# Two layers in one kernel on one core: first-round decays, one transform and the first trunk norm moved in their queues

## What is computed

```python
x = L0_attn_x                                   # 2 x 1024 tokens, 512 features, fp32
x = _layernorm(x + _L0_attn_ref(...))           # chunked linear attention with per-head decay,
                                                #   group RMS norm, sigmoid gate, Wo
x = _layernorm(x + _L0_ffn_ref(x, W1, W2, W3))  # silu(x W1) * (x W3), Hadamard transform of the
                                                #   2048 hidden features, W2
x = _layernorm(x + _L1_attn_ref(...))           # selective scan, 32 states for each feature
x = _layernorm(x + _L1_ffn_ref(...))            # silu(gate) * up, down
```

## Time and profile before

| | us |
|---|---|
| median of 3 runs | 1839.29 (1838.42 to 1845.17) |
| the profiled execution, its own time | 1843.79 |
| its span, first to last instruction | 1842.0 |
| TensorE busy | 1756.0 (95%) |
| VectorE busy | 1242.6 (67%) |
| ScalarE busy | 1119.2 (61%) |
| GpSimd busy | 1190.7 (65%) |

### The profile page before, as it was taken

How to read it: one execution, slowest core, us unless ns; L and a number is a source line. 1 busy time by engine, 2 the same in 40 slices (tenths; PEclk the granted TensorE clock), 3 DMA queues, 4 the chain that set the end, 5 groups by cost and what they waited for, 6 DMA issues and landing times. The chain is left out here.

```text
span 1842.0 us, 26738 instructions
## 1 busy us (share of the span) xinstructions
PE 1756.0 (95%) x9472; PEld 1132.3 (61%) x9472; DVE 1242.6 (67%) x1336; ACT 1119.2 (61%) x1721; POOL 1190.7 (65%) x932
## 2 busy tenths in 40 slices
PE   7898989889989999999999999998999999999998
PEld 5666656567756565555555665554655566667886
DVE  2524252423119999799888999887999999992212
ACT  5453444476567777777777777676776767663212
POOL 4534344255618887799976997788987888772111
PEclk9999999999989999999999999999999999999999
DMA  7433423387948988788776997677888777865662
GB/s 251 133 123 98 129 76 132 126 300 264 328 118 294 319 294 283 232 294 314 247 253 218 323 322 260 226 268 244 285 256 300 249 266 270 291 232 167 205 194 93
DMA packets 159222, 427.29 MB, mean 232 GB/s; under 512 B 30992, under 2 KB 54096, under 8 KB 158704
## 3 DMA queue, kind: packets, MB, share of 16 engines
q1 hardware_dynamic: 159088, 425.57, 68.8%
HBM read 356.30 MB, written 69.21 MB: 231 GB/s over the span
## 5 line engine op out<-in xcount | busy, mean ns | idle before, releaser
L1852 POOL TENSOR_TENSOR q_or_raw_or_h_times_c<-h_states,c_rep 128x512 f32<-128x512 f32 x293 | 375.7, 1294 | 82.0 <-DVE h_states L1745 52.7
L1622 ACT ACTIVATE decay<-delta_on_states,a_neg 128x512 f32<-128x512 f32 x512 | 350.7, 716 | 28.9 <-DMA delta_on_states<-delta 27.7
L1730 DVE TENSOR_TENSOR du_spread_in_d_b<-du_spread_in_d_b,b_rep 128x1024 f32<-128x1024 f32 x256 | 310.9, 1214 | 54.4 <-PE du_spread_in_d_b L1439 53.9
L1745 DVE TENSOR_TENSOR_SCAN h_states<-decay,h_last,du_spread_in_d_b 128x512 f32<-128x512 f32 x256 | 318.3, 1270 | 7.1
L1852 POOL TENSOR_TENSOR h_times_c_rest<-h_states,c_rep 128x512 f32<-128x512 f32 x219 | 280.8, 1293 | 61.3 <-DVE h_states L1745 40.5
L1745 DVE TENSOR_TENSOR_SCAN h_states<-decay,du_spread_in_d_b 128x512 f32<-128x512 f32 x256 | 302.6, 1209 | 14.7 <-ACT h_last L1627 7.8
L1804 POOL TENSOR_TENSOR h_lo<-v_or_silu_in_h_lo,h_hi 128x512 fp32r<-128x512 f32 x128 | 166.2, 1299 | 177.8 <-ACT h_hi L1524 177.6
L111 PE MATMUL y_or_aux<-h_hi,w 128*128 128x512 f32 x468 | 222.4, 475 | 10.1 <-POOL h_lo L1804 8.8
L1439 PE MATMUL du_spread_in_d_b<-stack,selectors 96*128 96x512 bf16 x512 | 200.6, 392 | 0.3 <-DVE h_states L1745 0.3
L1524 ACT CAST h_hi<-v_or_silu_in_h_lo 128x512 fp32r<-128x512 f32 x128 | 78.9, 616 | 180.9 <-DVE v_or_silu_in_h_lo L1695 180.8
L1695 DVE TENSOR_TENSOR v_or_silu_in_h_lo<-v_or_silu_in_h_lo,up_or_scores 128x512 f32<-128x512 f32 x128 | 86.7, 677 | 146.2 <-PE up_or_scores L113 133.4
(11 more groups left out here) (240 smaller groups left out, 3863.5 us busy)
## 6 DMA issues: line engine op xcount, KB each, us to landing
delta_on_states<-delta SPq DMA_DIRECT2D x256, 512.0 KB, 5.9
w<-w_split SPq DMA_DIRECT2D x112, 512.0 KB, 5.6
attn_w_hi_or_x_hi_w<-w_split SPq DMA_DIRECT2D x112, 512.0 KB, 5.4
attn_w_lo_or_x_lo_w<-w_split SPq DMA_DIRECT2D x112, 512.0 KB, 5.5
w_split<-w_presplit_hi_lo SPq DMA_DIRECT2D x32, 512.0 KB, 3.6
w_presplit_hi_lo<-in_w13b SPq DMA_DIRECT2D x32, 256.0 KB, 3.7
w_split<-attn_w_hi_or_x_hi_w SPq DMA_DIRECT2D x8, 1024.0 KB, 6.7
w_split<-attn_w_lo_or_x_lo_w SPq DMA_DIRECT2D x8, 1024.0 KB, 6.3
```

What stands on the lines that cost most here:

```text
L1622: act.activation(da[:, s % ND], dring[:, s % NR], ACT.Exp, scale=a[:, column(s):column(s) + 1]).then_inc(s_da, 1)
L1730: dve.tensor_tensor(both, both, brep[:, tile_of(s // SPO) % 2].unsqueeze(1).to_broadcast([P, 2, TT]), ALU.mult).then_inc(s_db, 1)
L1745: dve.tensor_tensor_scan(hs[:, s % NH], da[:, s % ND], uu[:, s % NU], initial, ALU.mult, ALU.add).then_inc(s_hs, 1)
L1852: pool.tensor_tensor(hc[s % NC_], hs[:, s % NH], crep[:, tile_of(s // SPO) % 2], ALU.mult).then_inc(s_hc, 1)
```

## The change

Four places are edited.

**Round 0.** `had0` comes behind the first two `k` groups. ScalarE's head decays, 5 before the second weight's hi part and 11 behind the first `v` group before, now stand at 1, 3, 1 and 7 between and behind the first hi parts, and the last 4 with the column decays behind the fourth `q` group. The second weight's hi part is made behind the first `q` group is taken.

**Rounds 1 to 3.** `take_transformed(1)` is split: first half, hi part 0 of the normed output, second half, hi parts 1 to 3. VectorE's lo parts follow one by one behind the four keys that it takes out.

**Constants.** The sum weights and epsilon (129 columns) get a buffer of their own, shared by both phases, and a transfer of their own; the trunk's two memsets and the wait for them are gone.

**Trunk.** The first norm's variance sums are issued at ticks 21 and 24, instead of 16 and 19.

```diff
-        FIRST = (["q"] * KD + ["had0"] * 2 + ["k"] * KD + ["v"] * CPT + ["gate"] * KD + ["had1"] * 2
+        FIRST = (["q"] * KD + ["k"] * 2 + ["had0"] * 2 + ["k"] * 2 + ["v"] * CPT + ["gate"] * KD + ["had1"] * 2
                  + ["kT"] * CPT)
...
-                sp.dma_start(const[:, :], cn).then_inc(s_const, 16)
+                sp.dma_start(const[:, :], cn[:, 0:C_SUM]).then_inc(s_const, 16)
+                sp.dma_start(ones[:, :], cn[:, C_SUM:CW]).then_inc(s_const, 16)
...
                     if rd.first:
-                        pe.wait_ge(s_const, 16)
+                        pe.wait_ge(s_wl, 2)
+                        for m in range(2):
+                            project("k", 1, m, xh, xl)
+                        pe.wait_ge(s_const, 32)
                     transform(0)
...
                         for k in range(KD):
                             act.wait_ge(s_x0[k], 16)
                             act.copy(xh[:, k], x[:, k, 0:TT]).then_inc(by_piece(k, s_xh, 1, p_xh)[0], 1)
+                            decays_of_heads(HEADS[k:k + 3] if k == 1 else [])
                             act.wait_ge(s_w0[k], 16)
                             act.copy(aw_hi[:, 0, k], raws[0][:, k]).then_inc(by_piece(k, s_wh, 1, p_wh)[0], 1)
-                        decays_of_heads(HEADS[:5])
-                        weight_high(1)
-                        decays_of_columns()
+                            decays_of_heads(HEADS[0:1] if k == 0 else HEADS[4:5] if k == 2 else [])
+                        decays_of_heads(HEADS[5:12])
...
-                    take("q", qT, ACT.Silu, ms=range(2))
+                    if rd.first:
+                        take("q", qT, ACT.Silu, ms=range(1))
+                        weight_high(1)
+                    take("q", qT, ACT.Silu, ms=range(1 if rd.first else 0, 2))
...
                     take("q", qT, ACT.Silu, ms=range(3, KD))
+                    if rd.first:
+                        decays_of_heads(HEADS[12:])
+                        decays_of_columns()
+                        take("k", kT, ACT.Silu, ms=range(2))
                     take_transformed(0)
...
-                    take("v", v, ACT.Silu, ms=range(1))
-                    if rd.first:
-                        decays_of_heads(HEADS[5:])
-                    take("v", v, ACT.Silu, ms=range(1, KD))
+                    take("v", v, ACT.Silu)
...
+                    take_transformed(1, range(1))
                     if not rd.first:
-                        high_of_normed()
+                        high_of_normed(range(1))
...
-                    take_transformed(1)
+                    take_transformed(1, range(1, 2))
+                    if not rd.first:
+                        high_of_normed(range(1, KD))
...
-                    if not rd.first:
-                        low_of_normed()
...
                         dve.tensor_tensor(kd[:, c, :], rd.bank("kT", c), kdec[:, :], ALU.mult)\
                            .then_inc(s_dt, 1)
+                        if not rd.first:
+                            low_of_normed(range(c, c + 1))
...
-VAR_PARTS_TICK = (16, 48, 105, 210, 281, 306, 402, 461, 498, 549, 594, 663, 690, 777)
-VAR_TICK = (19, 53, 105, 212, 283, 308, 404, 465, 500, 551, 596, 663, 692, 777)
+VAR_PARTS_TICK = (21, 48, 105, 210, 281, 306, 402, 461, 498, 549, 594, 663, 690, 777)
+VAR_TICK = (24, 53, 105, 212, 283, 308, 404, 465, 500, 551, 596, 663, 692, 777)
...
-                    if e == 0:
-                        pe.wait_ge(s_cm, 2)
...
-                dve.memset(ones[:, 0:P], 1.0 / HD).then_inc(s_cm, 1)
-                dve.memset(eps, EPS).then_inc(s_cm, 1)
```

More of the change, by code:

```diff
@@ L59 @@
 CW = C_EPS + 1
+S_EPS = C_EPS - C_SUM
 SLOTS = 3
@@ L83, in __init__ @@
         self.first = p.sb("q_or_raw_or_h_times_c", [P, KD, TT])
+        self.ones = p.sb("sum_weights_eps", [P, CW - C_SUM])
         with ExitStack() as same_memory:
@@ L124, in attention_phase @@
         p = Prog(nc, ctx)
-        const = p.sb("const", [P, CW])
+        const, ones = p.sb("const", [P, C_SUM]), joint.ones
         pre = p.sb("w_presplit_hi_lo", [P, SLOTS, 2, TT])
@@ L368, in mean_parts @@
                         for k in range(KD):
-                            mm = pe.matmul(out[k * HD:(k + 1) * HD, :], const[:, C_SUM:C_SUM + HD], x[:, k, tok(t - 2)],
+                            mm = pe.matmul(out[k * HD:(k + 1) * HD, :], ones[:, 0:HD], x[:, k, tok(t - 2)],
                                            tile_position=(0, k * HD))
@@ L377, in square_parts @@
                             pe.wait_ge(s_lq, KD * (t - 2) + k + 1)
-                            mm = pe.matmul(out[k * HD:(k + 1) * HD, :], const[:, C_SUM:C_SUM + HD], lsq[:, k],
+                            mm = pe.matmul(out[k * HD:(k + 1) * HD, :], ones[:, 0:HD], lsq[:, k],
                                            tile_position=(0, k * HD))
@@ L385, in sum_of_parts @@
                         pe.wait_ge(*rd.out(parts))
-                        pe.matmul(out, const[:, C_SUM:C_SUM + P], part[:, :]).then_inc(s_pj, 1)
+                        pe.matmul(out, ones[:, 0:P], part[:, :]).then_inc(s_pj, 1)
                     def norms():
@@ L505, in body @@
                         sum_of_parts("vb", "vp")
-                    for m in range(KD):
+                    for m in range(2 if rd.first else 0, KD):
                         project("k", 1, m, xh, xl)
@@ L610, in head_rstd, with high_of_normed, take_transformed @@
                             act.activation(lsq[:, 0], lsq[:, 0], ACT.Exp, scale=-0.5).then_inc(s_lr, 1)
-                    def high_of_normed():
+                    def high_of_normed(ks=range(KD)):
                         act.wait_ge(s_pj, rd.base if rd.tail else rd.done("v", CPT - 1))
-                        for k in range(KD):
+                        for k in ks:
                             act.wait_ge(s_on, KD * rd.prev + k + 2)
                             act.copy(onh[:, k], on[:, k]).then_inc(s_oh, 1)
-                    def take_transformed(i):
-                        for half in range(2):
+                    def take_transformed(i, halves=range(2)):
+                        for half in halves:
                             act.wait_ge(s_pj, rd.done(f"had{i}", half))
@@ L811, in scale_x, with low_of_normed @@
                             dve.tensor_tensor(xt, xt, lsq[:, 0], ALU.mult).then_inc(s_ln, 1)
-                    def low_of_normed():
-                        for k in range(KD):
+                    def low_of_normed(ks=range(KD)):
+                        for k in ks:
                             dve.wait_ge(s_oh, KD * rd.prev + k + 1)
@@ L1116, in trunk_phase @@
         a = p.sb("a_neg", [P, KD * SPO])
-        ones = p.sb("sum_weights_eps", [P, P + 1])
+        ones = joint.ones
         stk = joint.stack
@@ L1134, in trunk_phase @@
         yb = p.ps("scan_y", [P, TT])
-        s_const, s_a, s_cm, s_keep = (p.sem(n) for n in ("scan_const_in", "a_ready", "sum_weights_ready", "keep_ready"))
+        s_const, s_a, s_keep = (p.sem(n) for n in ("scan_const_in", "a_ready", "keep_ready"))
         s_g, s_u, s_sg = joint.g, joint.u, joint.sg
```

7 lines of the change are left out of this document (2 added, 5 removed).

## The result

The changed kernel took 1846.9 us (median of 8 runs, 1844.97 to 1848.95), the kernel before 1840.75 (8 runs beside them, 1837.69 to 1845.17). The ratio is 1.0031, with a 95% interval of 1.0020 to 1.0043. The forecast was 1839.2, a change of -0.1 us, with a range up to 1844.5. The median lies 7.7 us above the forecast and 6.1 above the kernel before, so the forecast was wrong. The profiled execution took 1847.54 us against 1843.79, with a span of 1845.8 against 1842.0, at a mean clock of 0.992 against 0.990: these two are only 3.75 us apart, since the profiled execution of before was one of its slower ones.

What follows compares the result with a forecast made beforehand. TensorE was taken to bound the kernel, busy 1756.0 of 1842.0 us. Terms of -1.8, -0.6, 0 and +2.3 gave -0.1 us on the median of 1839.29, so 1839.2 us, with an 8-in-10 range of 1830 to 1844.5.

Steps and rivals of the forecast that it cites:

- round 0: First attention round: -5.9 us from removed waits and clock, +2.8 waiting for butterflies, +1.3 clock fall; -1.8 us in all.
- rounds 1 to 3, order: Later attention rounds: transposes start sooner, but VectorE's queue limits the gain to 0.2 us a round, 0.6 in all.
- constants: Sum weights' 1.4 us wait between the phases: barrier stays and ScalarE's queue sets what follows; 0 us (0 to 1.4).
- trunk head: First trunk norm: gain at tick 16 lost at tick 24, behind chunk 5's cast that waits for a store; +2.3 us.
- The queue on VectorE takes the place of the wait: Rounds 1 to 3, before the output projection: three keys and two interleaved lo parts end at 133.6; 0.2 us won a round.
- the rule for it: VectorE with two SBUF operands delays GpSimd: in round 0, 1.94 us per meeting with a butterfly, 3.9 us charged for two.
- both waits: Round 0, TensorE's waits for the first query and value groups: 2.7 and 1.8 us, both to go, 4.5 us.
- the fall at 20 to 25 us: Round 0, clock at mean grant 0.66 behind the query wait; 1.7 us lost, taken as won without that pause.
- the bound of 3.8 for GpSimd: Round 0, upper bound on the wait of `had1` for GpSimd's butterflies, forecast at 2.8 us, lower bound 0.
- B: Rival: round 0 keeps its gain because VectorE hardly holds GpSimd, trunk gives nothing; -6.5 us, 1832.8; chance 0.18.
- C: Rival: every named wait goes, -16 us, 1823; chance 0.09, all cases under 1830 together.
- D: Rival: slower through the variance behind chunk 5's cast, store 4 us later and clock falls; +9.0 us, 1848.3; chance 0.13.

Runs made afterwards that it cites:

- e8: Kernel before with only the new order of high and low parts around the transform in rounds 1 to 3: 1841.62 us, 1.0004.
- e9: Kernel before with only the constants for the sums in a shared buffer of their own: 1844.28 us, 1.0022.
- e7: Kernel before with only the first trunk norm's sums moved to ticks 21 and 24: 1844.93 us, 1.0023.
- e10: e6 with the constants back in their old place: 1835.36 us, 0.9966 to the kernel before.
- e6: Changed kernel, GpSimd's blocks held behind the low parts (rounds 1 to 3), sums at 16 and 19, round 0's VectorE work off the butterflies: 1838.64 us, 0.9983.
- e3: Changed kernel with the trunk sums at 16 and 19 and the old order of rounds 1 to 3: 1843.29 us, 0.9998 to the kernel before.
- e12: Kernel before with only the first round's new order, constants in their old place: 1842.30 us (11 runs), 0.9999.

## Why the prediction was wrong

The ledger of the parts, each as it was measured:

| step of the forecast | forecast, us | measured, us | from |
|---|---|---|---|
| round 0 | -1.8 | -1.25; -1.5 between means | ledger; 4 executions with the old order, 7 with the new |
| rounds 1 to 3, order | -0.6 | +2.0 (3 x 0.68) | e8, 1.35 in two rounds |
| constants | 0 | +0.8 (3 x 0.27) | e9, 0.55 in two rounds |
| trunk head | +2.3 | +2.5 | ledger; 3.0 in e7, 3.4 on average over the four kernels with 21 and 24 |

**The step that failed** is "The queue on VectorE takes the place of the wait. I win 0.2 a round". Its sum was right up to the first key bank: the output projection started 0.27 us earlier. What it left out is where the low parts now stand in time. Until the change they were over at 131.35 (128.85 + 2.50, rows 10), and GpSimd's blocks started at 132.39. Moved behind the keys, the last two run beside them and take 1.71 and 1.18 us instead of 0.62; the last ends at 135.6, and the product that needs it starts at 135.66. The forecast had the rule for it, and used it for round 0 alone. Without the meeting (e10 against kernels with the old order) the step is worth -0.55 a round, more than the 0.2.

**Round 0** held in its mechanism: both waits gone, full clock from 15 to 50, 0.28 us ahead of `had0`, GpSimd's start 1.4 us later, `had1` at 55.9 (55.4) with 2.37 us (2.8), the clock at 0.66 behind it. Two gaps are left. TensorE was to come to `had1` at 52.6, and came at 53.55: the slower pace up to 15.55 us (0.7) and that of the values (0.15) had no term. A wait that was shorter by 0.4 us made up for part of it, and that is luck. And the fall at 20 to 25 us, counted as 1.7 us to be won, is not there in every execution of the old code.

**Constants** at 0: right for the wait and the barrier, wrong for the whole, by a route that no row of before showed. **The trunk head** held in place and cause, and in size in this execution; the same ticks cost 2.5 to 4.7 us in four kernels, since the store and the clock's falls lie differently in each. Of the range, the bound of 3.8 for GpSimd had its place, but rounds 1 to 3 had "0 to 3" for a gain and nothing for a loss. **Rivals**: B and C fell with the wait at 55.92 and with the Silu queue. D ended on the right side for another reason than its store landing late.

The parts add up to -1.5 + 2.0 + 0.8 + 2.5 = 3.8 us, up to 4.8 with the 3.4 that the four kernels with 21 and 24 average at the trunk head. The interval of the measured ratio begins at 3.7. The rest, up to the 6.1 between the medians, isn't resolved: the clock's falls move from execution to execution, and each is worth 1 to 2 us. What the constants cost in all stays open as well. Three pairs of kernels differ in them alone. By their ratios they cost 4.1 us in e9 against the kernel before, 3.1 in e6 against e10, and nothing (-0.2) in e3 against e12, each give or take 3; the ledger has 0.8.

The Trainium skill ("SBUF — State Buffer", Who interferes with whom) has a VectorE instruction with two SBUF inputs and a GpSimd one that reads SBUF exclude each other, the later one blocking fully. By that a 0.68 us low part behind a 1.29 us subtraction takes, as an estimate, up to 1.97; it took 1.71. The trace agrees, with each engine in turn the later one. In round 1 GpSimd's first subtraction ended at about 133.3 and the low part at 133.91; the second subtraction ended at 135.05 and the last low part at 135.61. At 40 us GpSimd's first ended at 40.91, VectorE's at 43.06 and GpSimd's second at 44.20. So both engines lose (3.33 and 3.07 us at 40 us). For table loads the trace has 1.28 us again, both times in round 0 (24.62 and 27.83), with the next activation right behind; a 2.66 us switch ("ScalarE: Activation LUTs", What ACT_TABLE_LOAD costs) does not appear, and the 0.28 us ahead of `had0` leave no room for it. ScalarE in the changed kernel:

```profile
24.62 1.28 ACT L569 ACT_TABLE_LOAD   x1
25.92 1.28 ACT L569 ACTIVATE decay_st<-w_presplit_hi_lo,attn_small 128x128 f32<-128x128 f32 x4
...
27.83 1.28 ACT L578 ACT_TABLE_LOAD   x1
29.12 1.09 ACT L578 ACTIVATE kT<-proj 128x512 f32<-128x512 f32 x2
```

## What to carry to other kernels

When an operation moves within its own queue, look at what the other engines do at its new time, not only at what it waits for; here a VectorE low part beside GpSimd's subtractions took 2.5 times as long. An ordering by ticks is priced by what it puts behind a waiting instruction: one tick, on the other side of a cast that waits for a store, was worth over 1.5 us. Effects under 1 us are read from the same instruction in several timelines, one part at a time, and against more than one execution of the kernel before.

## What the runs showed of the hardware

TensorE's value products came every 2.80 us instead of 2.75 in each kernel where the 129 columns of constants had a buffer of their own, whatever else was changed, at full clock and without waits (9 kernels); in the 5 without it, 2.75. What in that edit slows these products is not known.

VectorE operations with two SBUF inputs and GpSimd's subtractions take turns and so lengthen each other, 1.29 to 3.33 us and 2.29 to 3.07 us in the same meeting. One with an input in PSUM kept its 0.68 us. TensorE's clock can fall to 1.2 GHz (0.50 in windows of 1 us) behind a wait of 1.40 us, but not behind each. In the six kernels with the old order of rounds 1 to 3 it fell behind 3 of 18 such waits for `had_b`; with the new order, where the wait is 0.63 us, behind none of 24. Behind the same wait of 2.1 us in the tail it fell in the changed kernel and not in the one before.
